# Two fused attention and expert layers on one core: the expert stage written out tile by tile, and its results stored one group later in SP's queue

## The reference, cut to what matters

```python
logits = einsum('sbd,de->sbe', x, Wg) + bg + bias
vals, idx = top_k(logits, 2)
w = softmax(vals - max(vals))
h = relu(einsum('sbd,edh->esbh', x, W1) + b1)     # W1: 16 x 128 x 256
y = einsum('esbh,ehd->esbd', h, W2) + b2          # W2: 16 x 256 x 128
out = einsum('esbd,sbe->sbd', y, cw)              # cw: w at the two chosen experts, else 0
```

## Time and profile before

| | us |
|---|---|
| runs shown | 1195.06, 1191.57, 1212.96 |
| their median | 1195.06 |
| the profiled execution | 1195.27 |
| its span | 1193.4 |

### The profile page before, as it was taken

The page is one execution under the profiler, slowest core; times in us unless marked ns, Lnnn a source line. Parts: engine busy times, 40 slices in busy tenths (PEclk is TensorE's granted clock), DMA queues, the critical chain, the costliest instruction groups (busy, mean ns, idle before and its releaser), DMA issues. The chain is left out here.

```text
span 1193.4 us, 41254 instructions
## 1 busy us (share of the span) xinstructions
PE 1052.4 (88%) x13498; PEld 848.3 (71%) x13499; DVE 822.2 (69%) x2573; ACT 588.0 (49%) x1415; POOL 648.9 (54%) x1155
## 2 busy tenths in 40 slices
PE   4999999979999993898899996899999999998893
PEld 4788787856877772677777784677777777776672
DVE  1777777786777776444444445678888888887784
ACT  2666666644656651334344441335555454544454
POOL 2333333324777776666620004467777777777755
PEclk9999999998999997899999997999999999999997
DMA  3321122222334201244343332111111111111101
GB/s 73 86 50 43 38 52 69 68 66 70 98 90 104 70 23 39 86 125 122 111 112 88 88 88 58 32 29 36 43 41 45 40 45 39 45 41 40 41 23 31
DMA packets 106888, 74.21 MB, mean 62 GB/s; under 512 B 21360, under 2 KB 98288, under 8 KB 106736
## 3 DMA queue, kind: packets, MB, share of 16 engines
q1 hardware_dynamic: 98544, 55.40, 17.9%
q0 software_dynamic: 8192, 16.79, 4.7%
HBM read 38.60 MB, written 33.55 MB: 60 GB/s over the span
## 5 line engine op out<-in xcount | busy, mean ns | idle before, releaser
L659 ACT ACTIVATE arena<-PS 77x512 f32<-77x512 f32 (+4 forms) x736 | 305.1, 441 | 464.5 <-PE PS L1177 270.7
L1177 PE MATMUL PS<-arena 128*32 128x128 f32 (+5 forms) x9488 | 452.9, 291 | 50.2 <-issue 16.6
L1177 PEld LDWEIGHTS PS<-arena 128*32 128x32 f32 (+4 forms) x9488 | 352.4, 145 | 129.4 <-issue 36.5
L1177 PE MATMUL PS<-w,arena 128*128 x960 | 199.8, 325 | 9.0 <-issue 7.1
L521 POOL DMA_INDIRECT moe_rows<-arena x128 | 127.4, 996 | 71.7 <-POOL arena L517 50.3
L1177 PEld LDWEIGHTS PS<-w,arena 128*128 128x128 f32 x960 | 135.5, 195 | 29.8 <-issue 17.8
L640 POOL TENSOR_TENSOR arena<-arena,minus_half 128x2 f32<-128x2 f32 (+1 forms) x71 | 51.2, 721 | 189.4 <-DVE arena L1156 185.5
L598 POOL DMA_INDIRECT arena<-moe_results,slot x128 | 128.7, 1005 | 43.8 <-issue 31.6
L536 POOL TENSOR_TENSOR arena<-arena,minus_half 128x2 f32<-128x2 f32 (+1 forms) x70 | 47.6, 680 | 187.9 <-DVE arena L834 166.4
L1057 DVE TENSOR_TENSOR arena<-PS,b_rows 128x256 f32<-128x256 f32 x160 | 67.8, 424 | 90.0 <-PE PS L1177 74.4
L1177 PEld LDWEIGHTS PS<-arena,wk_wq 128*128 128x128 f32 x512 | 80.4, 198 | 45.5 <-issue 43.0
(11 more groups left out here) (151 smaller groups left out, 1657.9 us busy)
## 6 DMA issues: line engine op xcount, KB each, us to landing
moe_rows<-zeros SPq DMA_DIRECT2D x64, 160.0 KB, 2.5
arena<-moe_rows SPq DMA_DIRECT2D x40, 256.0 KB
moe_results<-arena SPq DMA_DIRECT2D x40, 256.0 KB
residual<-in_x SPq DMA_DIRECT2D x64, 64.0 KB
w<-in_W SPq DMA_DIRECT2D x32, 128.0 KB
arena<-in_ctxC SPq DMA_DIRECT2D x64, 64.0 KB
out<-arena SPq DMA_DIRECT2D x64, 64.0 KB, 1.6
arena<-in_ctxT SPq DMA_DIRECT2D x32, 77.0 KB
```

The lines of the kernel that those rows point to most:

```text
L659: A.activation(o, i, ACT.Copy).then_inc(s[done], 1)
L1177: return T.matmul(o, l, r, start=start, stop=stop)
```

## The change

SP: the store of a group stands one group later in the queue. The order is now load g, store g-3, load g+1, store g-2; three stores are left behind the last load in place of two. Engines: the expert stage's 166 steps are written out on TensorE, DVE and ScalarE; there is no loop left in it. The last argument of `run_steps` (34, `LAST_LAG_B + 2`) makes steps 34 to 159 leave out the edge waits, as the loop did.

```diff
-        def spans(count, lead, lag):
-            return [(0, lead, True), (lead, count, False), (count, count + lag, True)]
-
...
                 for g in range(c * NG_B, c * NG_B + 4):
                     load_group(c, g, g % 2)
-                    if g >= 2:
-                        store_group((g - 2) // NG_B, g - 2, g % 2)
+                    if g >= 3:
+                        store_group((g - 3) // NG_B, g - 3, (g - 3) % 2)
                 with sp.Fori(c * NG_B // 2 + 2, (c + 1) * NG_B // 2) as turn:
                     for p in range(2):
                         load_group(c, turn * 2 + p, p)
-                        store_group(c, turn * 2 + (p - 2), p)
-            for g in range(NCH * NG_B - 2, NCH * NG_B):
+                        store_group(c, turn * 2 + (p - 3), 1 - p)
+            for g in range(NCH * NG_B - 3, NCH * NG_B):
                 store_group(NCH - 1, g, g % 2)
...
-            for span in spans(NCH * NT, LOOPB, LAST_LAG_B):
-                run_steps(pe, NCH * NT, *span, step_b, LOOPB)
+            run_steps(pe, NCH * NT, 0, NCH * NT + LAST_LAG_B, True, step_b, LOOPB, LAST_LAG_B + 2)
...
```

More of the change, by code:

```diff
@@ L726, in step_b @@
                     cp(xsT[t.par(0)], PS[:, t.par(0), 0:D], "xsT_cp")
-            for span in spans(NCH * NT, LOOPB, LAST_LAG_B):
-                run_steps(act, NCH * NT, *span, step_b, LOOPB)
+            run_steps(act, NCH * NT, 0, NCH * NT + LAST_LAG_B, True, step_b, LOOPB, LAST_LAG_B + 2)
             act.wait_ge(s["w1_loaded"], 16 * len(loads1))
@@ L1058, in step_b @@
                                     b1s[:, bass.ds(e, 1), :].rearrange("q o h -> q (o h)"), ALU.add).then_inc(s["h_made"], 1)
-            for span in spans(NCH * NT, LOOPB, LAST_LAG_B):
-                run_steps(dve, NCH * NT, *span, step_b, LOOPB)
+            run_steps(dve, NCH * NT, 0, NCH * NT + LAST_LAG_B, True, step_b, LOOPB, LAST_LAG_B + 2)
             def step_c(t):
```

## The result

The changed kernel takes 1173.59 us, the median of four runs (1172.85 to 1175.44), against 1193.42 for the kernel before (four runs, 1191.57 to 1212.96): ratio 0.984, interval 0.9816 to 0.9867. Predicted were 1177.5 us with a range of 1171 to 1188.

A forecast was written before the change was run, and what follows sets the result against it. Late group loads behind SP's stores and loop starts bound the expert stage's second half, GpSimd's scatter its first. Terms -4.9 (d), -15.1 (c), +3.0 (e), -0.8 (f) make -17.8: from 1195.27 to 1177.5 us, range 1171 to 1188.

The forecast's parts named there:

- (a): SP's queue: loads issued 3 steps earlier, 5 steps (6.0 us) before use, so the waits go; stores cost nothing.
- (b): Expert stage's loop starts: 1.8 us more at each of two places in the second half, gone once written out.
- fourth rival: SP's loads stay late; second half loses only its loop starts, gaining 3.6 us; 1189 us in all, chance 0.04.
- (c): Second half, tiles 80 to 159: 113.2 us falls to 98.1 at 4.92 us per four tiles, gain 15.1 us.
- (e): TensorE's clock after the wait before tile 80: drops to 0.50, costing 3.0 us, bounds 0 and 4.3.
- (d): First half: GpSimd's scatter keeps its pace, tile 80 starts at 599.5 instead of 604.40 us, gain 4.9 us.
- (f): From tile 159 to the last stage: the loop exit's table reads go away, gain 0.8 us, bounds 0 and 1.
- (g): Fetching the written-out code: 8 more packets in the second half, costed at nothing because fetched ahead of use.
- The step does not return: Expert stage: loads no longer late, but groups take 5.4 us rather than 4.92; 1187 us in all, chance 0.15.
- No wait for the scatter: Tile 80 follows tile 79 at 583 us: 16.5 us more gained, no clock lost; 1158 us, chance 0.05.
- Instruction fetch is the new bound: TensorE, second half: no gain from 2.2 us a packet on; 1221 us at 5.5 us each, chance 0.04.
- Loads are still late: SP's queue is held by a store wait one place further, second half keeps its waits; 1189 us, chance 0.04.

The follow-up runs named there:

- e1: The kernel before with only SP's new load and store order, its loops kept: 1145.31 us, ratio 0.9936 to the kernel before.
- e2: The changed kernel with SP's old order put back, so only the stage written out: 1153.35 us, ratio 0.9992 to the kernel before.
- e4: The changed kernel with the second chunk's scatters written out and reading rows and positions in place, without copies: 1113.47 us, ratio 0.9661 to the kernel before.
- e7: The changed kernel with 96 unread matmuls on TensorE ahead of the wait for tile 80's load: 1133.63 us, ratio 0.9851 to the kernel before.
- e8: The changed kernel with ScalarE and VectorE back in their loops, TensorE still written out: 1138.00 us, ratio 0.9877 to the kernel before.
- e3: The changed kernel without every second scatter of the second chunk (result not the program's): 1113.39 us, ratio 0.9663 to the kernel before.
- b1_before: The kernel before, unedited, run again on a chip of the follow-up runs: 1153.45 us, ratio 1.0002.
- a1_after: The changed kernel, unedited, run again on the same chip as b1_before: 1135.41 us, ratio 0.9848 to the kernel before.
- e6: The kernel before with the second chunk's scatters reading rows and positions in place, the edit of e4: 1151.42 us, ratio 0.9988 to the kernel before.
- e9: The changed kernel with SP's old order and ScalarE and VectorE in their loops, TensorE alone written out: 1151.80 us, ratio 1.0001 to the kernel before.

## Why the prediction was right, and where it was off

**(a) and the load of a group: right.** SP's loads go out 5.6 us ahead of use, against a forecast of five steps, 6.0; the 12 waits are gone; VectorE never waited for the store. e1 does this part alone and shows the waits gone with the loops in place.

**(b), the loops: right in place, too small in size.** I priced a loop return at 1.8 us, as the difference between a held-up group and one with a return. Against a plain step the return cost more once nothing else held it: in e1 the two groups at the first return of the second half take 6.50 and 5.82 us where plain ones take about 4.95, together 2.4 us, and those at the second 6.39 and 7.24, together 3.7. At the second the clock also dipped (0.50 from 662.2 to 665.6); the second costs 1.3 us more. A read of the table is 0.30 us on TensorE (median of 54 in e1), and no instruction packet is near the second return, so code that had to be fetched is not what it waits for. In the kernel before, part of this hid behind the late load. The sum was not hurt, since it went by whole groups and not by this figure, but the "3.6" of the fourth rival rested on it and on the belief that the two parts add. e2 measured what that rival's place would give without the order: in the second half not 3.6 us gained but 2.3 lost.

**(c), the second half: the mechanism was right, the term was 1.2 us too small.** It took the plain group at 4.92 us from the earlier trace rows; written out it is 4.83. The 79 steps as e4 and e7 show them are 95.6 us, where 97.2 stood as the best case. The difference of 0.09 a group is TensorE's own loop: plain groups take 4.92 to 4.97 us in e1 and 4.83 in e8, which differ in this half in TensorE's code alone. It is probably the register work around the table read; that part was only argued. The added delay was 0.9 us; tiles 91 and 92 show 1.3 (1.93 and 1.81 less 2.42), and the later profiles none. So 96.9 us before the clock's 2.7, where 98.1 stood: 1.6 us too much for the steps, 0.4 too little for the delay. Written as the prediction has it, (c) and (e) together were -15.1 + 3.0 = -12.1; measured -13.6.

**(d), tile 80: right.** Forecast 599.5, it came at 598.97: the load left 0.3 us earlier than I had allowed and was used 2.7 us after, not 2.9. The wait of 11 to 20 us was 15.0 as counted. e3 and e4 show that only the scatter stood behind it, and how much was buried in it: 20.7 us of first half and the restart. In b1_before and a1_after the same term is 1.8 us, because there the kernel before waited for the scatter as well.

**(e), the clock: right.** 3.0 us forecast, 2.7 in the profile (tiles 80 to 84 in 7.57 us where 4.83 is plain) and 2.8 by e7. That the value taken lay so near is in part luck: it was chosen between bounds of 0 and 4.3. The clock was at 0.50 from 587.4 to 604.5, but only the part behind tile 80 counts, 5.5 us of it, at half speed: 2.8. By the Trainium skill (TensorE: Matmul & The Clock Gate, HAM oscillation), whose penalty is half of the throttled time, this is just what should come out; the 4.2 us that I worked out with it used a throttled stretch of 8.5 us from the stage's beginning, and that length, not the rule, was wrong here.

**(f) and (g): right.** The exit gave 0.9 us for 0.8. Eight packets of TensorE's instructions came in in the second half, the number forecast, and no issue idle of 1 us is there. That they cost "nothing" holds for this kernel with 5.6 us for a load; in e2, with 3 us, four of the five long loads stand beside such packets. The cover is the early load, which the prediction had not named.

**The rivals.** "The step does not return" gave 1187 and fails on the 4.83 us group. "No wait for the scatter" fails on the kernel as it is, and is what e4 makes true: its 22 us are near the 19.5 (16.5 and the clock's 3.0) at which this rival was priced, though with a longer wait to take away than in the first comparison. "Instruction fetch is the new bound" needed 2.2 us a packet, and the longest idle of TensorE for issue in the second half is 0.4 us. "Loads are still late" fails on the trace at tile 132.

The total: 17.8 us forecast, 19.7 measured. Of the 1.9 us between, 1.5 are (c) with (e), 0.4 are (d) and 0.1 (f), each rounded.

## What to carry to other kernels

When two faults overlap in one loop (a late load and slow loop turns), price them together and as whole periods: in the second half the order alone was worth 7 us and the written-out code alone less than nothing, both together 15. Ask of every stage that gets faster what fixed pace it now runs into; here a shorter scatter on GpSimd, worth next to nothing ahead of the change (ratio 0.9988 in e6), was worth 22 us behind it. In an issuing queue put what is wanted soonest first, and move a store behind the load that does not need it.

## What was not expected of the hardware

Copies and waits between indirect DMAs cost more than they look: GpSimd's scatter of a pair went from 3.55 to 2.53 us once it read rows and positions in place, with the same 0.96 us for the DMA instruction itself. Copies, their wait and the loop went together in e4 and were not tried apart.

Instruction packets of 16 KB share the DMA engines with data. Of the loads that take 3.8 us or more in the second half of e2 and e9, where 2.9 is usual, six have one in flight beside them (4.5 us for the load at 634.30 in e2) and two have GpSimd's gathers instead. No run isolates either.

One and the same kernel differs by 33.6 us in one stage, the last, between the first comparison (466.4 us) and b1_before (432.8), while the ratios of the change are alike, 0.984 and 0.985. In the longer one TensorE stood idle for issue for 16.6 us. Whether the chip makes the difference or something else was not tried.
